# Newton roots of the layer-norm variances: seven batches moved from GpSimd to VectorE

## The reference

```
mod = (silu(c) @ wmod).reshape(32, 6, 1, 128)
sa, ca, ga, sb, cb, gb = six parts of mod      # ga, gb: magnitude at least 0.25, sign kept
h = layernorm(x) * (1 + ca) + sa
x = x + ga * scan_block(h)      # g, a = sigmoid(h Wg + bg), sigmoid(h Wd + bd); v = h Wv + bv
                                # s_t = a_t s_(t-1) + (1 - a_t) v_t along the sequence; result s * g
h = layernorm(x) * (1 + cb) + sb
x = x + gb * moe(h)             # 8 experts 128 -> 512 -> 128 with relu, top 2 by softmax of the gate
layernorm(x) = (x - mean) / sqrt(var + 1e-5) over the 128 features
```

## Time and profile before

| | |
|---|---|
| median of 3 runs | 508.05 us (507.99 to 511.54) |
| the profiled execution | 513.39 us, its span 511.6 us |
| DVE busy | 445.7 us (87%), 1291 instructions |
| TensorE busy, matmuls | 419.9 us (82%) |
| ScalarE busy | 300.3 us (59%) |
| POOL busy | 210.5 us (41%), 293 instructions |
| mean granted clock of TensorE | 0.898 of full speed |

### The profile page before, as it was taken

One profiled execution on the slowest core, in us unless ns is written; L12 is line 12 of the kernel. 1 busy time (PEld: TensorE's weight loads), 2 busy tenths in 40 slices (PEclk: granted clock), 3 DMA queues, 4 the chain that ended last, 5 costly groups with the idle time before them and its releaser, 6 DMA issues.

```text
span 511.6 us, 14923 instructions
## 1 busy us (share of the span) xinstructions
PE 419.9 (82%) x4291; PEld 344.3 (67%) x4292; DVE 445.7 (87%) x1291; ACT 300.3 (59%) x756; POOL 210.5 (41%) x293
## 2 busy tenths in 40 slices
PE   2856989887888611999999999999999998998960
PEld 2424555545557510799999888899888888888850
DVE  5889899987889784999999999999999999999960
ACT  1537897958695400577666666666665666555520
POOL 6043342777726773033343433334434333333331
PEclk9989897987785555899999999999999999999985
DMA  7534452533313343223323332223333222222210
GB/s 233 150 112 138 140 176 88 187 141 126 119 69 125 142 156 117 56 80 80 84 79 99 84 94 77 77 77 86 82 95 87 61 71 73 73 74 74 68 39 0
DMA packets 48137, 51.03 MB, mean 100 GB/s; under 512 B 5454, under 2 KB 41759, under 8 KB 48082
## 3 DMA queue, kind: packets, MB, share of 16 engines
q1 hardware_dynamic: 39968, 33.17, 23.3%
q0 software_dynamic: 7040, 16.93, 9.2%
q10 hardware_dynamic: 1074, 0.23, 0.2%
HBM read 27.43 MB, written 24.70 MB: 102 GB/s over the span
## 4 chain that ended last, share of the span: by engine, by line
DVE 30%; issue 25%; PE 24%; POOL 14%; DMA 2%; ACT 1%; DVEq 1%; SPq 1%; POOLq 1%; ACTq 0%
POOL sorted_rows L539 12%; DVE xs L1164 8%; PE bank L1401 3%; PE bank L1404 3%; PE bank L1402 3%; DVE hT L1177 3%; PE bank L1385 3%; PE bank L1387 3%; PE bank L1386 3%; DVE a L1182 2%; DVE xn L875 2%; DVE tg L1185 2%; DVE st L815 2%; PE bank L1262 2%; DVE w2f L1166 1%
## 5 line engine op out<-in xcount | busy, mean ns | idle before, releaser
L559 POOL DMA_INDIRECT out_dram<-tg,midx x92 | 106.3, 1155 | 199.2 <-DVE tg L1185 185.2
L718 ACT ACTIVATE xs<-bank,bcols 128x256 f32<-128x256 f32 x368 | 139.6, 489 | 32.6 <-PE bank L1387 32.2
L1401 PE MATMUL bank<-w2hi,xs 128*128 x736 | 122.7, 220 | 0.0
L1402 PE MATMUL bank<-w2hi,w2f 128*128 x736 | 122.7, 220 | 0.0
L1166 DVE TENSOR_TENSOR w2f<-xs 128x1024 f16<-128x1024 f32 x92 | 112.7, 1225 | 3.2
L1404 PE MATMUL bank<-w2lo,xs 128*128 x736 | 101.9, 220 | 0.0
L1385 PE MATMUL bank<-xh,w1hi 128*128 128x256 f16 x368 | 101.5, 276 | 0.3 <-ACT xs L718 0.3
L1386 PE MATMUL bank<-xl,w1hi 128*128 128x256 f16 x368 | 101.3, 275 | 0.0
L1387 PE MATMUL bank<-xh,w1lo 128*128 128x256 f16 x368 | 101.3, 275 | 0.0
L539 POOL DMA_INDIRECT sorted_rows<-pay,idx x64 | 63.9, 998 | 30.6 <-issue 19.0
L1402 PEld LDWEIGHTS bank<-w2hi,w2f 128*128 128x128 f16 x736 | 72.6, 99 | 0.0
(11 more groups left out here) (220 smaller groups left out, 710.1 us busy)
## 6 DMA issues: line engine op xcount, KB each, us to landing
xs<-sorted_rows SPq DMA_DIRECT2D x46, 260.0 KB, 2.9
xs<-sorted_rows SPq DMA_DIRECT2D x47, 128.0 KB, 2.5
sorted_rows<-padt SPq DMA_DIRECT2D x10, 582.0 KB, 5.2
w2f<-in_L_ffn_w_dram SPq DMA_DIRECT2D x4, 512.0 KB, 4.7
xs<-in_L_ffn_w_dram SPq DMA_DIRECT2D x4, 512.0 KB, 3.9
xs<-in_L_attn_x_dram SPq DMA_DIRECT2D x3, 512.0 KB, 8.5
out_dram<-tg,midx POOLq DMA_INDIRECT x92, 3.1
sorted_rows<-pay,idx POOLq DMA_INDIRECT x64, 2.7
```

The lines of the kernel that those rows point to most:

```text
L559: pool.indirect_dma_start(out_rows, bass.IndirectOffsetOnAxis(midx[k][:, t:t + 1], 0), yout[k][:, t, :], None, bounds_check=TOK - 1, oob_i ...
L718: ins = act.activation(hf[e][:, cc, :], bank[2 * e + cc // 2][:, (cc % 2) * TW:(cc % 2 + 1) * TW], ACT.Relu, bias=bcols[n % 2][:, e * HC + ...
L1401: pe.matmul(o[t], hh[n % 2][e][:, cc, t * P:(t + 1) * P], whi, start=False, stop=False)
L1402: pe.matmul(o[t], hl[n % 2][e][:, cc, t * P:(t + 1) * P], whi, start=False, stop=False)
```

## The change

`QUICK` names all 13 batches instead of six, so that `variances` on DVE makes every root and POOL's `scales` is called for none. The waits on `slow_scales` and `var_ready` fall away with it, since `scaled` then waits on `quick_scales` for each batch. The place of each `variances` in DVE's order, and of each scatter in POOL's, is the same.

```diff
-QUICK = (0, 1) + tuple(range(len(BATCHES) - 4, len(BATCHES)))
+QUICK = tuple(range(len(BATCHES)))
```

## The result

The changed kernel takes 521.41 us (median of 4 runs, 518.61 to 522.02), the kernel before in the same round of runs 509.8 us (4 runs, 507.99 to 515.4). The ratio is 1.0198, 95% interval 1.0104 to 1.0292. Run again later it was 1.0202 (1.0146 to 1.0257), with medians of 540.55 against 528.31 us. So the change makes the kernel 2% slower. The direction was forecast with 0.75; the time, 515.7 us with a range from 511.0 to 519.5, was too low.

A forecast was written before the change was run, and what follows sets the result against it. VectorE (DVE) was taken to bound the front: 13.9 us of added root steps minus 6.2 us of waits given back is 7.7 us, on a 508.05 us median 515.7 us, with an 8-in-10 range of 511.0 to 519.5.

The forecast's parts named there:

- the bound: In the front DVE is the bound, POOL its servant; the end is idx of super-group 4 plus about 31 us.
- the price of a step: Each dependent root step on DVE costs 0.206 us alone, 0.12 us beside another chain.
- the base: The 508.05 us median to which the forecast added its loss; the profiled execution took 513.39 us.
- the list of what comes back: DVE waits in turns 4, 11 and 12 that vanish: 1.6, 3.3 and 1.3 us, together 6.2 us.
- cheap-step rival: In the front, dependent steps on DVE cost only 0.12 us: +2.2, 510.3 us; chance 0.12.
- Partners: Batches 2 to 7 pay all ten steps alone, 2.06 us each; batch 8 pays six alone and four beside choose.
- the three turns: Turns 4, 11 and 12, where DVE waits of 1.6, 3.3 and 1.3 us were to come back.
- the sum of 7.7 us: Net loss over the front: 13.9 us of added DVE steps minus 6.2 us of waits given back.
- clock rival: TensorE stays longer at its lower clock, three more slow projection turns adding 4.2 us: +11.9, 520 us; chance 0.08.

The follow-up runs named there:

- the fourth round: The changed kernel with a fourth Newton round for batches 2 to 8 on DVE, 21 more dependent steps: 527.06 us, ratio 1.0317 to the kernel before.
- Batch 7 alone: The kernel before with only batch 7's roots moved from POOL to DVE: 513.28 us, ratio 1.0053; again in a later round 536.34 us, ratio 1.0087.

## Why the prediction was right and wrong

The direction, the bound and the price of a step were right. Two terms failed: the base, a median of three runs that was 3.6 us too low, and the list of what comes back, which left no room for new waits. The first is the larger part of the miss in time.

**Bound.** Right. The end of the front is `idx` of super-group 4, at 174.40 us (173.5 forecast), the last scatter ends at 205.4 us (204 forecast), the rest is unchanged at 314.8 us.

**Price of a step.** Right, by the batches in the trace and by the fourth round. The cheap-step rival is out. The Trainium skill ("VectorE: DVE Perf Modes", section "The DRAIN you can't avoid") says that a semaphore between chained operations costs nothing extra. I took from it that a step behind the one that it waits for would cost what a paired one does. The rows disagree with that reading: 0.2 us right behind the step before, 0.12 beside another narrow chain, 0.07 between statistics. No run here takes the semaphore out of a lone chain, so the page's own sentence is not tested.

**Partners.** Right: only batch 8 had any, and it paid 1.08 us where I had 1.5. Added in all 13.4 us instead of 13.9.

**What comes back.** In the trace the three turns gave 6.7 us (6.2 forecast). The step that failed is that I took this list as complete, as if all else stayed where it was. Turn 9 took 3.9 us, turns 13 and 14 returned 1.3, and a start that happened to be 0.6 us earlier makes up the rest: 13.4 - 6.7 + 3.9 - 1.3 - 0.6 = 8.7 us, against 8.6 measured. So the sum of 7.7 us came within 1 us of the trace partly by luck: the named terms were 1.0 us smaller than forecast (13.4 - 6.7 against 13.9 - 6.2), and the unnamed ones added 2.0 us. Batch 7 alone shows the same weakness: 2.0 us paid and 3.8 us given back in its trace, yet 0.5% and 0.9% slower in two rounds of runs. The clock rival named this kind of loss (projections at 3.4 instead of 2.0 us in more of the turns where TensorE comes last), and its 520 us is nearest to the measured time. In the first trace its mechanism is there, in turn 9 alone and not in the three turns that it priced. In the second trace the same wait came from pauses of ScalarE. That the change itself brings the lower clock about is not shown.

**The base.** The sum was made against the profiled 513.39 us, and there it would have given 521.1; measured was 522.02. I then set it on a median of three runs, two of which belong by their times to the fastest group. The prediction saw the 5.3 us between the two and said that the loss could be larger in the usual run, but gave this no term. The changed kernel's four runs had clocks of 0.896 to 0.908; only one of them reached the 0.907 at which that group begins. Of the 5.7 us between 515.7 and 521.4, 3.6 us is this base (508.05 against 511.7 in 23 runs). The other 2 us fit the waits above, which left the trace 0.9 us over the sum, but they are less than the interval of the ratio leaves open (0.0094, or 4.8 us, to either side).

**Checks that I named.** Lines 854 to 860 ran 39 times each, `nmr` of batch 7 was there 2.3 us after its seed, and the waits of turns 4, 11 and 12 are gone. New idle time of DVE above 3 us, the sign of the clock rival, came in turn 9 and not in turns 12 to 14. Wrong was "20 us or more" of idle POOL ahead of super-group 3: 9.62 us, because the freed time fell ahead of super-groups 1 and 2.

**Open.** Why moving batch 7 costs the median run 2.7 to 4.6 us. The mean clock of the 12 runs of the first round was 0.900 against 0.903, worth 0.7 us by the slope above; in the one trace of that round the expert stage alone was 2.4 us longer; the rest has no name. Open too is what stops ScalarE in the pauses put down to "remote".

## What to carry to other kernels

Price a small dependent operation by who stands beside it: the same instruction cost 0.20 us alone, 0.12 us beside another narrow chain and 0.07 us between statistics (its width, 128x4 to 128x16, made no difference to the 0.20: in turn 12 of the kernel before two 128x4 steps start at 132.41 and 132.61 us). So place a chain where there are partners before moving it to a busier engine. When a wait is removed, walk on to the next guard (shared buffers, queue order) and ask who now arrives first; its slack in the old trace is the limit of the gain. And set a sum on runs of the same clock as the trace that it was worked out from.

## What the hardware showed that I had not expected

The kernel before, unchanged, fell into groups 2 to 3 us apart in one round, ordered by the mean granted clock (0.917, 0.901 to 0.91, 0.894 to 0.898, 0.885). The same kernel had medians of 511.7, 528.31 and 533.04 us in the three rounds, which the record puts on three chips. All eight traces of the two longer rounds have waits of over 1 us put down to "remote" or "issue" between 100 and 190 us, of VectorE up to 4.9 us and of ScalarE up to 11.8 us; the first two traces and the four of the first round have none between 20 and 190 us. And six small matmuls per turn, about 0.5 us together, put where TensorE mostly had to wait anyway, cost 5 to 10 us.
